# Where ScalarE keeps the scan's last column, and where VectorE takes the statistics, in a Mamba layer's scan

## The reference

```python
def step(h, inp):
    u_t, d_t, b_t, c_t = inp
    dA = jnp.exp(d_t[..., None] * A)
    dBu = (d_t * u_t)[..., None] * b_t[:, None, :]
    h = dA * h + dBu
    y = jnp.einsum('bdn,bn->bd', h, c_t)
    return (h, y)
...
y = y + u * D_skip
y = y * jax.nn.silu(z)
out = y @ out_proj_w.T          # 1024 -> 512 channels
...
x = x + out                     # then a group norm for layer 1
```

## Time and profile before

| | |
|---|---|
| median of three runs | 5062.46 us |
| the profiled execution's own time | 5062.96 us |
| its span | 5061.3 us |
| TensorE busy | 4610.7 us (91%) |
| VectorE busy | 4117.5 us (81%) |
| ScalarE busy | 2978.4 us (59%) |
| GpSimd busy | 3411.0 us (67%) |

### The profile page before, as it was taken

How to read it: one execution, slowest core, us unless ns; L and a number is a source line. 1 busy time by engine, 2 the same in 40 slices (tenths; PEclk the granted TensorE clock), 3 DMA queues, 4 the chain that set the end, 5 groups by cost and what they waited for, 6 DMA issues and landing times. The chain is left out here.

```text
span 5061.3 us, 120130 instructions
## 1 busy us (share of the span) xinstructions
PE 4610.7 (91%) x47160; PEld 2959.7 (58%) x47160; DVE 4117.5 (81%) x4324; ACT 2978.4 (59%) x6070; POOL 3411.0 (67%) x1712
## 2 busy tenths in 40 slices
PE   5999999993899999999999999999999699999899
PEld 4666666662455545555555555555554588887787
DVE  7888888863999999999999999999998577776332
ACT  2666666664776767667776676677664445543211
POOL 0577767776999989989999999899998122222000
PEclk9999999996999999999999999999999799999999
DMA  5344444433223332333233323332331111111443
GB/s 199 114 150 150 151 150 146 150 134 116 83 75 94 94 94 77 94 94 93 77 94 94 93 77 94 94 93 77 93 93 58 71 75 75 75 75 62 195 195 137
DMA packets 191783, 538.35 MB, mean 106 GB/s; under 512 B 15824, under 2 KB 15840, under 8 KB 181840
## 3 DMA queue, kind: packets, MB, share of 16 engines
q1 hardware_dynamic: 185920, 480.31, 28.0%
q0 software_dynamic: 5104, 51.35, 2.5%
q10 hardware_dynamic: 288, 0.00, 0.0%
HBM read 329.22 MB, written 202.38 MB: 105 GB/s over the span
## 5 line engine op out<-in xcount | busy, mean ns | idle before, releaser
L919 POOL TENSOR_TENSOR sc_hc<-sc_hc,sc_c_rep 128x1024 f32<-128x1024 f32 x1024 | 2389.8, 2371 | 255.2 <-ACT sc_state L940 254.0
L1154 DVE TENSOR_TENSOR_SCAN sc_hc<-sc_da,sc_state,sc_ring 128x512 f32<-128x512 f32 x2048 | 2443.8, 1259 | 131.1 <-PE sc_ring L1064 115.2
L979 ACT ACTIVATE sc_da<-sc_delta,l_neg_a 128x512 f32<-128x512 f32 x2048 | 1351.3, 707 | 0.0
L1064 PEld LDWEIGHTS sc_ring<-sc_diag,sc_dut 64*64 64x64 f32 x32768 | 890.1, 133 | 620.0 <-issue 618.7
L1074 PE MATMUL sc_y_ps<-sc_hc,sc_fold 128*64 128x512 f32 x4096 | 994.5, 606 | 157.1 <-POOL sc_hc L919 150.4
L1064 PE MATMUL sc_ring<-sc_diag,sc_dut 64*64 64x128 f32 x32768 | 1074.7, 274 | 20.5 <-DMA sc_w_out<-in_w_out 16.8
L940 ACT ACTIVATE sc_state<-sc_hc 128x2 f32<-128x2 f32 x1024 | 204.8, 200 | 640.1 <-DVE sc_hc L1154 636.8
L1074 PEld LDWEIGHTS sc_y_ps<-sc_hc,sc_fold 128*64 128x64 f32 x4096 | 249.2, 136 | 553.4 <-issue 348.0
L1084 PE MATMUL sc_o_ps<-sc_yg,sc_w_out 128*128 128x512 f32 x1024 | 524.3, 617 | 2.9 <-ACT sc_o_sb L963 2.1
L1362 POOL TENSOR_TENSOR l_count<-l_count,as_oh 128x1024 f32<-128x1024 f32 x64 | 182.6, 2853 | 508.2 <-DVE as_oh L1545 508.2
L71 PE MATMUL fr_mm<-fr_xn_hi,l0f_w_in_hi 128*128 128x512 f32 x1024 | 437.1, 427 | 26.3 <-DVE fr_delta L671 11.8
(11 more groups left out here) (166 smaller groups left out, 6429.2 us busy)
## 6 DMA issues: line engine op xcount, KB each, us to landing
sc_duz<-spill SPq DMA_DIRECT2D x128, 768.0 KB, 5.7
sc_delta<-spill SPq DMA_DIRECT2D x256, 256.0 KB, 4.0
spill<-fr_z SPq DMA_DIRECT2D x64, 512.0 KB, 2.8
spill<-fr_u SPq DMA_DIRECT2D x32, 1024.0 KB, 8.7
spill<-fr_du SPq DMA_DIRECT2D x32, 1024.0 KB, 4.3
spill<-fr_delta SPq DMA_DIRECT2D x32, 1024.0 KB, 6.4
sc_c_rep<-bc SPq DMA_DIRECT2D x128, 256.0 KB, 4.1
soft<-as_et SPq DMA_DIRECT2D x16, 2048.0 KB, 6.3
```

Of the source, the lines that this page charges most:

```text
L919: nc.gpsimd.tensor_tensor(hc[:, p], hc[:, p], c_rep[:, 2 * q:2 * q + 2, :], ALU.mult).then_inc(s_hp, 1)
L979: nc.scalar.activation(da[:, p % 4, r, :], delta[:, i % 2, p % 2, :], ACT.Exp, scale=keep.neg_a[:, c:c + 1]).then_inc(s_da, 1)
L1064: done = nc.tensor.matmul(to[:, :, k::4], dut[rows, i % 2, k, HALF * h:HALF * h + HALF], diag[rows, u, 4 * q + c:4 * q + 4:2, k, :], start ...
L1154: nc.vector.tensor_tensor_scan(hc[:, p, r, :], da[:, p % 4, r, :], ring[:, SLOT[at], r::2], state[:, i, 2 * p + r:2 * p + r + 1], ALU.mult ...
```

## The change

Two things are moved, in ScalarE's and in VectorE's order. On ScalarE, the group in front of the decays of pair 5 (keep_column, keep_turned, write_skip) now stands ahead of keep_state of pair 2, where it stood behind it. This holds for all 128 blocks. On VectorE, the statistics of a projection part are taken behind the second scan of pair 4 in the even blocks 0, 2, 4 and 6, where they were taken behind pair 3 of the odd block that follows. No instruction is added or taken away, and TensorE's, GpSimd's and SyncE's orders stay as they are.

```diff
@@ scalar body @@
                     for p in range(PAIRS):
-                        if p >= AHEAD:
-                            keep_state(g, i, p - AHEAD)
-                        elif i:
-                            keep_state(g, i - 1, p + PAIRS - AHEAD)
-                        elif past:
-                            keep_state(g - 1, KD - 1, p + PAIRS - AHEAD)
                         if p == 5:
                             if i == 0 and more:
                                 keep_column(g + 1)
...
                             write_skip(g, i, i + 1 < KD or more)
+                        if p >= AHEAD:
+                            keep_state(g, i, p - AHEAD)
+                        elif i:
+                            keep_state(g, i - 1, p + PAIRS - AHEAD)
+                        elif past:
+                            keep_state(g - 1, KD - 1, p + PAIRS - AHEAD)
                         decays(g, i, p)
@@ vector body @@
                         recur(g, i, p, 1)
-                        if p == 3 and i in (3, 5, 7) and past:
+                        if p == 4 and i in (2, 4, 6) and past:
                             statistics(*past[0], i // 2 - 1)
-                        if p == 3 and i == 1 and len(past) > 1:
+                        if p == 4 and i == 0 and len(past) > 1:
                             statistics(*past[1], KC - 1)
```

## The result

The changed kernel took 5245.45 us (median of four runs, 5241.9 to 5251.91) against 5060.23 for the kernel before in the same runs. The ratio is 1.0373, with a 95% interval of 1.0351 to 1.0396: 185 us slower. The forecast was 5240.

What follows compares the result with a forecast made beforehand. A loop through TensorE, ScalarE and GpSimd, three nearly full engines, was taken as the bound. 59 even blocks x 1.99 plus 68 others x 0.86 made 176 us on 5062.96, rounded to 5240; range 5205 to 5290.

Steps and rivals of the forecast that it cites:

- The bound: Scan blocks: a loop turn, keep_turned, write_skip, keep_state, GpSimd, add_up, fills, turn sets the time; 21.32 us even, 20.44 odd.
- The ScalarE edit: All 128 blocks: GpSimd's pair 2 starts at 2.20, pair 3 at 4.52 instead of 3.66 us; loop 0.86 us longer.
- The VectorE edit: 59 even blocks: VectorE stands 3.88 us for add_x; the even block is 1.99 us longer, both edits together.
- the statistics' start: Even blocks, VectorE: statistics start 1.30 us after add_x's start at 6.83, so at 8.13 us behind the turn.
- The sum: Whole program: 59 x 1.99 = 117 and 68 x 0.86 = 58 us, 176 us in all, giving 5239, rounded to 5240.
- The range's upper end: Whole program: 5290 us, given for up to 1.1 us in the other blocks and 2.9 in the even ones.
- The stall in full: Rival: no gap takes anything up, even blocks lose 0.86 + 4.46 us, the others 0.86; 5435 us; 5%.
- the VectorE edit alone as the cost: Rival: lateness of GpSimd's pair 3 is absorbed, even blocks take 1.13 us more; 5130 us; 7%.
- faster: Rival: statistics leave the odd block and fill a wait in the even one, if add_x started by 2.95; 5028 us; 3%.
- the clock: Rival: TensorE waits more and its granted clock falls to a mean of 0.95, 127 us on top; 5367 us; 3%.
- no effect: Rival: neither move, on ScalarE or VectorE, is on the path; the time stays at 5063 us; 2%.

Runs made afterwards that it cites:

- the fifth experiment: keep_state of pair 3 moved directly behind write_skip, ahead of the decays of pair 5, on the kernel before: 4949.77 us against 5065.24, ratio 0.9771.
- the first experiment: ScalarE's reorder alone, VectorE's order as in the kernel before, against the kernel before: 5175.49 us against 5067.44, ratio 1.0218.

## Why the prediction was right

- *The bound.* A loop through TensorE, ScalarE and GpSimd: shown from both sides in the chunks with projections. What delays GpSimd's pair 3 lengthens the blocks, and what brings it forward shortens them, until TensorE has no gap left.
- *The ScalarE edit.* 0.86 us a block were forecast for 2.20 and 4.52 us behind the turn. The changed kernel has pair 2 at 2072.56 - 2070.36 = 2.20, and odd blocks of 21.29 in place of 20.44: 0.85. Over the program 109 us were expected of it alone and 110 measured. For the blocks of chunk 0 this was in part luck. Their 0.86 was taken from rows of another chunk, though VectorE had no gap in chunk 0 and might have covered a part of the delay. They went from 19.26 to 20.11 us all the same, while an earlier pair 3 won nothing there (the fifth experiment): so VectorE and the loop through GpSimd must have been about equally long there, and no row of the prediction shows that.
- *The VectorE edit.* The stall was forecast at 3.88 and is 4.01 us in the block shown, and longer in the first block of a chunk (4.71 in the next chunk). The even block was forecast at 1.99 more and shows 2.15 (23.47 against 21.32), which is also the mean over 58 even blocks. The undersized term is the statistics' start. It was put at 1.30 us behind add_x's start, from the four cases behind the last block. That holds for 19 of the 59 statistics within the blocks; for the other 40 it is 1.41 (2077.22 to 2078.63, and see the last section). In an even block of chunk 8, one of the 19, the statistics start 8.15 us behind the turn (8.13 forecast), and the block lasts 23.35 us where it lasted 21.35: 2.00 more, for 1.99. In the chunks with 1.41 the like block has 2.12 more. The first block of a chunk gets 2.36 more (23.55 against 21.19), which the sum didn't set apart; it had been shorter than the other even ones.
- *The sum.* With 2.15 it reads 59 x 2.15 + 68 x 0.85 = 185 us, and the median moved by 185. That the two agree to the microsecond is luck: from the first keep_turned to the last the profiled executions differ by 184 us, their spans by 188.9. Two figures of the recorded working are off. The range's upper end doesn't follow from its own bounds, since 59 x 2.9 + 68 x 1.1 gives 5309 and not 5290; and reckoned by spans the ScalarE term would add 127 x 0.05 = 6 us, not 5. Neither touches the forecast.
- *Rivals.* The stall in full (5435) failed, since of 4.6 us of stall and statistics in an even block 1.3 reached the next turn (2.15 - 0.86) and 3.3 went into waits that were there; the VectorE edit alone as the cost (5130) failed by the first experiment; faster (5028) failed because add_x was at 6.86 and not before 2.95; the clock stayed at 1.00 from 1400 to 2600 us, and its drops in chunk 0 cost 0.7 us each, far from the 127 us of that rival; no effect (5063) failed.

That even and odd blocks could be summed apart rested on each beginning in much the same state. The changed profile bears that out: the turns repeat at 21.3 and 23.5 us.

## What to carry to other kernels

In front of an in-order engine's wait, put the small copy whose data are already there and for which another engine waits; behind it, it inherits the wait. Before a consumer is moved ahead, add up where its producer stands in its own queue: here add_x was at 5.97 us, and VectorE asked at 4.25. Where three engines are over 90% busy, work moved into one's gap can be free (the 0.58 us of statistics behind pair 6), and a new wait in one's work is paid in part: of 3.13 us of stall and 0.58 of statistics 1.25 reached the next block.

## What was not expected of the hardware

The wait of VectorE for add_x ended 1.40 to 1.46 us behind add_x's start in 40 of the 59 cases within the blocks, and 1.29 to 1.32 in the other 19, as behind the last block, with add_x recorded at some 1.27 us in all. The 40 are those of chunks 2 to 7 and 10 to 13, which the program runs in a hardware loop; the 19 stand in chunks that are written out. One of the 19, in chunk 8:

```profile
2711.37 1.27 POOL L928 TENSOR_TENSOR sc_x_res<-sc_x_res,sc_o_sb 128x512 f32<-128x512 f32 x1
2712.68 0.70 DVE L1164 BATCH_NORM_STATS2 keep_stats<-sc_x_res 128x6 f32<-128x512 f32 x1 [4.10 <-POOL sc_x_res L928]
```

In the loop a register instruction stands in VectorE's queue ahead of the statistics. The view of L1164 has exactly 40 of them, with a median of 64 ns, and they begin only when add_x has ended. The 64 ns are about half of the difference. No run takes that instruction away by itself, so that it makes the whole difference isn't shown.

Where the loop starts over, three times in the scan (at chunks 4, 6 and 12), the block before lasts 24.9, 26.6 and 26.6 us in the changed kernel and 24.4, 25.8 and 25.7 before, where other steps into a chunk last 21.9 and 21.1. TensorE stands idle for 3.01 us in front of add_up 3 at 2293.31, though GpSimd's pair 7 had ended at 2289.78. The profile puts this wait down to "issue" or to a multiplication of GpSimd's; what is waited for stays open. The stop comes in all kernels alike, 2.9 to 3.5 us each time, and on top of it comes the clock. The steps into chunks 4 and 6 of the changed kernel:

```profile
1918.00:1943.00 25.00, 20.49 (x306) 11.28 (x306) 17.56 (x16) 13.27 (x28) 18.68 (x9) 1.00 0.45 131
2281.00:2307.00 26.00, 21.68 (x304) 11.90 (x300) 17.24 (x15) 13.27 (x28) 17.94 (x8) 0.93 0.46 122
```

Behind the second stop, not behind the first, the granted clock fell to its lower level. Over the ten kernels of this document there are 30 such restarts. In the ten where the clock stayed at 1.00 the block is 3.0 to 3.5 us longer than at other chunks of the same kernel, and in the twenty where it fell 4.6 to 6.2 us. Which of the two comes varies from trace to trace; the three restarts of a trace together cost between 12.3 and 15.5 us.
